# Moving a gate projection, a normalization and an activation between the slots of a hand-scheduled Mamba and mixture-of-experts sweep

## The reference, cut to what matters

```
h = layernorm(x) * (1 + ca) + sa
xb, zb = split(h @ in_proj_w)            # 256 + 256 channels
xb = silu(conv4(xb) + conv_b)            # causal, 4 taps
zb = silu(zb)
dt, B, C = split(xb @ x_proj_w)          # 16 + 16 + 16
dt = softplus(dt @ dt_proj_w + dt_proj_b)
for n in 16 states:                      # along 512 tokens, 256 channels
    h_n[t] = exp(dt[t] * A_n) * h_n[t-1] + dt[t] * B_n[t] * xb[t]
    y += h_n * C_n
x = x + ga * (((y + xb * D) * zb) @ out_proj_w)
h = layernorm(x) * (1 + cb) + sb
gate = softmax(h @ gate_w.T); pick the largest of 8 experts
x = x + gb * gate * (relu(h @ w1[e] + b1[e]) @ w2[e] + b2[e])
# then layer 1: layernorm, key features exp(dash - diag - max), key-value sums
```

## Time and profile before

| | |
|---|---|
| median of three runs | 3715.17 us (3712.8 to 3717.01) |
| the profiled execution | 3715.17 us |
| its span, first to last instruction | 3713.4 us |
| span of one steady step of the first sweep | about 126.3 us |
| first sweep | about the first 2150 us |
| busy in a steady step: TensorE / VectorE / ScalarE | 106.5 / 115.5 / 86.4 us |

### The profile page before, as it was taken

One profiled execution on the slowest core, in us unless ns is written; L12 is line 12 of the kernel. 1 busy time (PEld: TensorE's weight loads), 2 busy tenths in 40 slices (PEclk: granted clock), 3 DMA queues, 4 the chain that ended last, 5 costly groups with the idle time before them and its releaser, 6 DMA issues. The chain is left out here.

```text
span 3713.4 us, 53483 instructions
## 1 busy us (share of the span) xinstructions
PE 2966.5 (80%) x15912; PEld 2167.9 (58%) x15912; DVE 2826.3 (76%) x4814; ACT 1957.2 (53%) x4744; POOL 887.8 (24%) x590
## 2 busy tenths in 40 slices
PE   2486888788888878887889958888888888888886
PEld 1164565556555655565566726667666666666665
DVE  3999898989999999999999335666666666666664
ACT  3465767676766676676766434333333333333332
POOL 0433333333333333333333000111111111111111
PEclk6588999999999999999999979999999999999998
DMA  2000000000000000000000010000000000000000
GB/s 100 7 4 13 19 16 3 18 16 16 6 18 16 9 12 18 16 3 18 16 16 2 19 68 19 11 24 8 23 16 16 16 16 16 16 16 16 16 8 11
DMA packets 49771, 64.31 MB, mean 17 GB/s; under 512 B 3584, under 2 KB 36416, under 8 KB 49184
## 3 DMA queue, kind: packets, MB, share of 16 engines
q1 hardware_dynamic: 47392, 54.93, 4.6%
q10 hardware_dynamic: 2304, 8.46, 0.6%
HBM read 41.78 MB, written 21.60 MB: 17 GB/s over the span
## 5 line engine op out<-in xcount | busy, mean ns | idle before, releaser
L789 POOL TENSOR_TENSOR acc<-acc,zz 128x1024 f32<-128x1024 f32 x256 | 607.7, 2374 | 1064.4 <-DVE h L1104 998.2
L1104 DVE TENSOR_TENSOR_SCAN h<-dec,u 128x1024 f32<-128x1024 f32 x256 | 585.4, 2287 | 14.1 <-issue 4.8
L918 PEld LDWEIGHTS bank<-one_sb,hid 128*128 128x128 f32 x4096 | 478.1, 192 | 28.1 <-issue 15.4
L918 PE MATMUL bank<-one_sb,hid 128*128 128x128 f32 x4096 | 480.9, 275 | 12.4 <-ACT hid L654 12.4
L866 PE MATMUL bank<-S,pick_sb 96*128 96x512 bf16 x512 | 215.1, 425 | 275.0 <-DVE zz L1116 170.7
L622 ACT ACTIVATE dec<-dt,aneg 128x512 f32<-128x512 f32 (+1 forms) x512 | 341.0, 720 | 128.5 <-DVE h L1104 112.2
L158 POOL TENSOR_SCALAR n_ve<-n_mv 128x4 f32<-128x4 f32 x96 | 54.4, 567 | 1388.1 <-DVE n_mv L141 1388.1
L866 PEld LDWEIGHTS bank<-S,pick_sb 96*128 96x128 bf16 x512 | 51.3, 100 | 472.5 <-DVE zz L1116 214.5
L1116 DVE TENSOR_TENSOR zz<-h,bank 128x1024 f32<-128x1024 f32 x256 | 312.5, 1221 | 12.9 <-PE bank L866 2.8
L1097 DVE TENSOR_TENSOR u<-dtx,bank 128x1024 f32<-128x1024 f32 x256 | 310.0, 1211 | 3.3 <-issue 2.4
L654 ACT ACTIVATE hid<-banks,one_sb 128x512 f32<-128x512 f32 x304 | 208.6, 692 | 93.8 <-PE bank L918 75.5
(11 more groups left out here) (265 smaller groups left out, 7048.8 us busy)
## 6 DMA issues: line engine op xcount, KB each, us to landing
kv_dram<-Gs ACTq DMA_DIRECT2D x16, 516.5 KB, 3.0
kvl<-kv_dram SPq DMA_DIRECT2D x16, 516.5 KB, 3.6
xs<-in_x SPq DMA_DIRECT2D x16, 256.0 KB, 2.8
x<-in_x SPq DMA_DIRECT2D x16, 256.0 KB, 2.9
x_dram<-x SPq DMA_DIRECT2D x16, 256.0 KB, 2.1
h_dram<-hT SPq DMA_DIRECT2D x16, 256.0 KB, 2.0
h<-h_dram SPq DMA_DIRECT2D x16, 256.0 KB, 2.6
x2s<-x_dram SPq DMA_DIRECT2D x16, 256.0 KB, 2.7
```

The lines of the kernel that those rows point to most:

```text
L789: pool.tensor_tensor(acc[:, :, :], acc[:, :, :], zz[:, k % 2, :, :], ALU.add)\
L918: last = pe.matmul(bank1(f"down{e}")[:, j * D:(j + 1) * D], hid[:, e % 2, f, j * P:(j + 1) * P], w2[:, e, f, :], start=(f == 0), stop=(f = ...
L1104: dve.tensor_tensor_scan(h[:, :, :].rearrange("p g t -> p (g t)"), dec[:, k % 2, :, :].rearrange("p g t -> p (g t)"), u[:, :, :].rearrange ...
```

## The change

Pieces move to other slots, and some to another place within a slot; no arithmetic is changed.

- `in_z` (TensorE) from slots 2 and 3 to 5 and 6, `silu_z` (ScalarE) from 3 and 4 to 6 and 7. In bank 7 the logits now come ahead of z0 and z1.
- The gate: logits and `choose` from slot 5 to 4, `gate_exp` from 6 to 5.
- The input norm of n: statistics from slot 5 to 6, application, transposition (`turn1`) and `modulate1` from 6 to 7.
- `in_x` and the copies of x from slots 7 and 8 to 8 and 9, the convolution from 8 and 9 to 9 and 10.
- `silu_x` stays in slot 10, but moves from the first place of the slot on ScalarE to the last, behind relu 16 to 18, `decay(11)` and `key_exp(2)`.
- `round_rest` stays in slot 12, but moves behind `decay(13)`.

```diff
-            XIN = {7: 0, 8: 1}
-            CONV = {8: 0, 9: 1}
+            XIN = {8: 0, 9: 1}
+            CONV = {9: 0, 10: 1}
...
-            uses[7] = ["z0", "z1", "logits", "turn1", "x0", "x1", "xdbl", "dt0", "dt1"]
+            uses[7] = ["logits", "z0", "z1", "turn1", "x0", "x1", "xdbl", "dt0", "dt1"]
...
 (ScalarE)
-                            if a is not None and slot in (3, 4):
-                                silu_z(slot - 3, a)
-                            if n is not None and slot == 10:
-                                silu_x(n)
+                            if a is not None and slot in (6, 7):
+                                silu_z(slot - 6, a)
...
-                            if n is not None and slot == 12:
-                                round_rest(n)
                             if a is not None and slot + 1 <= NS - 1:
                                 decay(slot + 1, a)
-                            if b is not None and slot == 6:
+                            if b is not None and slot == 5:
                                 gate_exp(b)
                             if y is not None:
                                 if slot in EXPS:
                                     key_exp(EXPS[slot], y)
                             if n is not None:
-                                if slot == 6:
+                                if slot == 7:
                                     modulate1(n)
+                                if slot == 10:
+                                    silu_x(n)
                                 if slot == 12:
+                                    round_rest(n)
                                     magnitude(0, n)
...
 (GpSimd)
-                            if n is not None and slot == 5:
+                            if n is not None and slot == 6:
                                 norm_pool(pool, L1, half, n, passed)
...
 (TensorE)
-                            if b is not None and slot == 5:
+                            if b is not None and slot == 4:
                                 gate_logits(b, s)
...
-                            if a is not None and slot in (2, 3):
-                                in_z(slot - 2, a, s)
+                            if a is not None and slot in (5, 6):
+                                in_z(slot - 5, a, s)
...
-                                if slot == 6:
+                                if slot == 7:
                                     turn1(n, s)
...
 (VectorE)
-                                if slot == 5:
+                                if slot == 6:
                                     dve.wait_ge(*x_in(n, 16))
                                     norm_stats(dve, L1, xs, n, passed)
-                                if slot == 6:
+                                if slot == 7:
...
                                     norm_apply(dve, L1, xs, n)
...
-                                if slot == 5:
+                                if slot == 4:
                                     choose(b)
```

## The result

The changed kernel takes 3741.66 us (median of 4 runs, 3737.98 to 3744.9) against 3713.99 us before (4 runs). The ratio is 1.0074, with a 95% interval of 1.0055 to 1.0091: 0.7% slower. The span grew from 3713.4 to 3743.7 us.

The account below looks back on a forecast made before the run. VectorE, busy 115.5 of 126.3 us a step, was taken as the bound, tied to TensorE and ScalarE. +1.15 - 0.35 = +0.8 us a step, +10 us with the end steps, gave 3725 us; 8-in-10 range 3698 to 3748 us.

Parts of the forecast that it names:

- P: End of `downs(3)` on TensorE, which relu 20 and 21 wait for: forecast at 1766.7, old 1767.31.
- T: End of `downs(2)` on TensorE, which relu 16 to 18 wait for: forecast at 1751.75, old 1758.65.
- The 6.03 us that the schedule could give: VectorE's waits in a step: 2.33 us in slot 5, 3.35 in slot 12, 0.35 ahead of softplus in slot 16.
- Slots 2 to 5, a gain of 3.2 us: VectorE, per step: 2.33 us from the wait for key product 3, 0.9 us from a shorter one-hot in `choose`.
- Slots 6 and 7, nothing: ScalarE: the table loads `silu_z` brings there are covered and cost nothing; up to 2.56 us a step without cover.
- rival B: Clock falls in slots 8 and 10, or loads reach VectorE: +2.1 us a step, 3742 us; with C, chance 0.15.
- `silu_x` behind the relus, `x_proj` at T + 6.6: Slots 10 and 11: relus, `decay`, `key_exp`, a Silu load and `silu_x` take 6.5 us from T; `x_proj` starts at 1758.35.
- The fallen clock, 1.5 us: TensorE in slot 11: after standing 4 to 4.8 us, 3.3 us at half clock, put at 1.5 us.
- Slots 11 to 13, P + 7.9 to `split_low`: ScalarE's chain from P to `Rb` takes 7.9 us; `split_low` starts 1.15 us later, VectorE waiting some 4 us.
- A: No clock fall in slot 11, or an equally shorter chain to `round_rest`: 0.7 us a step faster, 3707 us; chance 0.28.
- C: Slot 5's gain does not come, its key product late for another reason: another +1 to +2 us a step; with B, 0.15.
- D: Gain holds and the chain in slots 10 to 13 is hidden: up to -3.2 us a step, 3673 us; chance 0.05.

Follow-up runs that it names:

- e3: Changed kernel with `silu_x` back first in slot 10 and `round_rest` back ahead of `decay(13)`, so only moves to other slots are left: 3622.06 us, ratio 0.9750.
- e7: Kernel before with only input norm, `turn1`, `modulate1`, `in_x` and convolution a slot later: 3667.64 us, ratio 0.9859.
- e6: e3 with the gate (logits, `choose`, `gate_exp`) back in slots 5 and 6: 3632.77 us, ratio 0.9769.
- e1: Changed kernel with `silu_x` back at the first place of ScalarE's slot 10: 3624.99 us, ratio 0.9756.
- e5: Kernel before with one edit, `silu_x` moved to the end of ScalarE's slot 10: 3836.75 us, ratio 1.0318.
- e4: Changed kernel with four added products on TensorE ahead of `x_proj`, which overwrites them: 3716.73 us, ratio 1.0001.
- e2: Changed kernel with `round_rest` back ahead of `decay(13)`: 3717.81 us, ratio 1.0008.

## Why the prediction was right in sign and short in size

The forecast was slower, 3725 us, with a chance of 0.45 for slower. Measured were 3741.66 us, within the range of 3698 to 3748 us. The rise is 27.7 us (30.3 us between the two profiled executions) where 10 were forecast.

Redone from the rows, the miss of 20 us between the profiled executions has these parts, each as a mean over the 13 steps: the stretch from `x_proj` to P 0.9 us a step (11 us), T 0.35 us (5 us), the chain behind P 0.15 us (2 us), less 0.1 us in slots 13 to 16 (1 us). The steps at the ends are the other 3 us.

- **The 6.03 us that the schedule could give.** Nearly. e3 gets 6.8 us a step out of the moved slots: the waits of 2.33, 3.35 and 0.35 us, 0.94 us of the one-hot, and 0.57 us of a wait for the output projection in slot 2 that I had not counted (it stands in the rows of e7 at 1275.01, and not in the step of e3), less 0.69 us that softplus waits there. That is 6.85 us.
- **Slots 2 to 5, a gain of 3.2 us.** Confirmed in size: no wait in slot 5, the one-hot at 0.19 us. One reason was half wrong: e6 and e7 have `choose` in slot 5 and the short one-hot as well, so it was the input norm's move alone that freed it. The lockout rule of the Trainium skill ("SBUF — State Buffer", "Who interferes with whom") agrees with both.
- **Slots 6 and 7, nothing.** Confirmed. The four table loads stand there in e3 too, and VectorE does not wait in these slots.
- **Slots 8 to 10, T at 1751.75.** Measured 1751.74 in the step shown, and 0.35 us later on average. TensorE stays at full clock in slot 10, as forecast. Foreseen by rival B alone was the half clock in slot 8 (1761.4 to 1764.6 in the step shown, longer in the step with T 0.8 us later). That T fits to a hundredth is luck of the step that was chosen.
- **`silu_x` behind the relus, `x_proj` at T + 6.6.** Confirmed: 6.63 us. e1 and e5 show that this placement alone costs 8.9 us a step in the changed kernel and 8.4 in the one before. No drain shows beside the loads of 1.28 us: the activation follows at once (1783.34 + 1.28 = 1784.62, start 1784.63). The Trainium skill ("ScalarE: Activation LUTs", "What ACT_TABLE_LOAD costs") gives one of about 1380 ns; the two loads in the chain would then have made `split_low` 2.8 us later, and the rows are the measure.
- **The fallen clock, 1.5 us.** This is the term that was mis-sized. That TensorE would stand for 4 us and fall to half clock was right. But the half clock lasts 6.8 us here, of which 3.4 to 6.2 us lie behind the start of `x_proj`, and over the steps the stretch from `x_proj` to P took 9.24 instead of 6.85 us: 2.4 us, 0.9 more than forecast. e4 measures the same cost by taking it away: 2.3 us. The forecast took the length from windows of 3.3 us, and the trace of the kernel before has a longer stretch too: the granted clock is 0.50 from 1682.60 to 1689.30. In the step with 1657.62 the idle time is 4.66 us instead of 4.19 us, since TensorE did not have to wait for `zz` behind its late T; `x_proj` starts at T + 6.63 us there as well (1657.62 - 1650.99).
- **Slots 11 to 13, P + 7.9 to `split_low`.** Measured 8.05. The wait of "some 4 us" at L1081 is 4.17 us. `round_rest` behind `decay(13)` costs 1.23 us of it.
- **The steps at the ends.** Step 0 +1.1 (+1 forecast), step 1 +2.6 (+1.5). Of step 15 the -0.8 us (-3) can't be told from what varies behind it.
- **The rivals.** A (no fall in clock) did not happen; e4, which makes it happen, took 3716.73 us instead of the 3707 us of A, with half clock from 1693.2 to 1699.7 and a new wait of 1.04 us in slot 4. B had another mechanism (the fall earlier, in slots 8 or 10) and the measured time, 3742 us. Its waits of about 1 us in slot 8 and the fall behind them are there, but they make T only 0.35 us later on average, not 1 to 1.5 us. B's time therefore fits by luck: of the 1.3 us a step by which its 2.1 us exceed the forecast's 0.8, 0.9 us came from the longer half clock in slot 11. C and D fall with the rows of slots 5 and 13.

What stays open: why the half clock behind the same idle time of 4.19 us is 6.8 us long in the changed kernel and about half as long in nearly every step of e2, and why it begins at another place of the idle time from step to step. Also not run is `silu_z` in slots 6 and 7 with the input norm left in slots 5 and 6: `turn1` follows z1 in bank 7 and would wait for the `silu_z` of slot 7, while ScalarE would stand at `modulate1` in slot 6, ahead of it. By the code that is a deadlock: with this order of bank 7 the move of `silu_z` needs that of the input norm.

## What to carry to other kernels

In a queue that runs in order, the place within a slot can be worth more than the slot: a piece that feeds another engine belongs ahead of pieces that wait for that engine's last product. Follow the chain from that product on through every piece of the queue, table loads included, and look what it ends in. Where it leaves TensorE idle for 4 us, count the wait and then the half clock behind it, as the stretch behind it took 9.2 us instead of 6.9 us here. Look in several steps, not in one, how long the half clock lasts and where it begins: half of its part behind the idle time is the cost. When a change bundles moves, take them apart before it is given up: without its two reorderings this one is 2.5% faster than the kernel before.

## What was not expected of the hardware

Adding 3.6 us of useless products to TensorE ahead of `x_proj` made the kernel 25 us faster (3741.66 to 3716.73 us), since the stretch behind them ran wholly at 2.4 GHz (granted clock 1.00), where 3.4 to 6.2 us of it had been at 1.2 GHz (0.50). And an equal idle time did not cost the same. e2 and the changed kernel, with idle times of 4.19 us (4.66 us in every third step of the changed one), took 8.40 us and, on average, 9.24 us for the same stretch of work. Within the changed kernel it took 8.60 and 9.91 us behind the same 4.19 us, as the half clock of 6.8 us began 3.4 us ahead of the end of the idle time in one step and 0.6 us ahead in the other. A fall did not need one wait of 4 us either: in slot 8 TensorE was at 0.50 from 1761.4, in the second of two waits of 1.33 and 1.41 us.
